# Sparse mixtures with 16-bit one-hot products and a reordered router; value products of self-attention over wide columns

## The chip, the cores and the metric

One Trainium2 chip, one core. The metric is the device time of one execution of the whole program in microseconds; the time before is the median of three runs, 3148.82 us (3148.0 to 3151.92).

## The reference

x has 2048 tokens (32 x 64) of 256 features. Four layers follow one another, each a cross-attention, a token mixer and a feed-forward part, each added to x. The change touches three of these twelve parts:

```
L0 feed-forward: shared SwiGLU (256 -> 512 -> 256) + 8 such experts, each token goes to the best 2
    probs = softmax(LN(x) @ wg.T); topw, sel = top_k(probs, 2); topw /= sum(topw)
    out = shared(x) + sum_e expert_w[:, e] * (silu(x @ g_e) * (x @ u_e)) @ d_e
L3 feed-forward: the same form, 7 experts of 256 -> 256 -> 256, the best 3, with biases on the choice
L1 mixer: self-attention, 32 heads of 8 with 8 key/value heads: q = X @ Wq.T + bq, v = X @ Wv.T + bv (64 columns)
```

## The kernel before, in words

All tensors stay transposed in SBUF: k.x and k.h are [128, 2, 2048] f32 (feature, half, token). T = 2048 tokens are NT = 16 tiles of P = 128 or NCH = 4 chunks of CH = 512. PE is TensorE, DVE VectorE, ACT ScalarE, POOL GpSimd, SP SyncE. Each stage is a block in which every engine has its own list of instructions, written out in order, with semaphores between them; a block ends when all engines have arrived.

`sparse_experts` (called by `moe_top2` for L0 with M = I/P = 4 hidden tiles, and by `moe_top3` for L3 with M = 2) has three blocks.

**The router's block** (prefix `L0r_`, `L3r_`). A layer norm in four chunks (`Norm.mean`, `var` on PE, `centre`, `scale` on DVE, `squares`, `inverse` on ACT) with one PSUM bank for the means and one for the variances; `Logits` multiplies by the router's weights, `turned` transposes. PE transposes h by tokens (L828), ACT copies it (L865), SP stores it as `rows_in` (L800), then loads the experts' weights. The shared expert runs chunk by chunk in `shared_pe`: for each hidden tile a gate and an up product (L724, 2 x 2 products of 512 columns, into one of two banks; hidden tile n waits for `hidden(n-2)` to have been read), then the down product (L731). ACT makes the silu (L738), DVE the product (`shared_hidden`, L743) and the addition to x (`shared_add`, L747). Between these, DVE carries the routing in the order of the dictionary `between`: `soften` (softmax), `pick(j)` (one-hot of the j-th choice), `gather_masks`, `weigh` (the weights of the choices), `place` (a slot for each token and choice: experts' tokens lie together in blocks of 128), `own_blocks` (each block's expert), `sort_out(j)` (L951 to L953: a one-hot of the row in the block, 128 x 16 x 128, and one of the block times the destination number). PE then multiplies these one-hots (L843, f32, 16 products for each choice), which gives for each slot the number of its row; `make_lists` (L957 to L964) turns it into `token_of` and `row_of`. L0 does three chunks of the shared expert here (LATE = 3), L3 all four (LATE = 4).

**The experts' block** (`L0b_`, `L3b_`): 39 and 54 blocks of 128 rows. POOL gathers rows by `token_of` (L1032, four buffers), PE warms up with three products of ones (L1084), transposes the rows (L1049), multiplies (L1063), transposes the hidden rows (L1071), projects (L1081); POOL scatters by `row_of` (L1037). Behind the blocks come the shared chunks from LATE on, and SP reloads the first rows of the result (L1023).

**The combination** (`L0c_`, `L3c_`): PE starts with products of ones (L1159, `2 if LATE < NCH else 8`), then adds the rows of each token by diagonal matrices of the weights (L1167), DVE adds to x (L1182).

`self_attention`, block `sap_`: PE makes the values token tile by token tile (L1861, 32 products with 64 columns), then queries and keys in a loop over the chunks (L1868), ACT adds biases (L1878), DVE spreads the values (L1895) over a tile that POOL has zeroed (L1883).

Of the kernel before, what the change touches and what calls it, by code (L numbers as in the profile page):

```python
# [20 lines left out]
ts = bass.ts  # L21
# [650 lines left out]
def sparse_experts(k, layer, E, I, top, biases):  # L672
# [7 lines left out]
    with ExitStack() as ctx:  # L680
# [10 lines left out]
        spare = sb(k, ctx, "rows", [P, max(NT * D, top * NT * P)])  # L691
# [8 lines left out]
        s_x = nc.alloc_semaphore(k.prefix + "rows_stored")  # L700
        rows_in = nc.dram_tensor(k.prefix + "rows_in", (T, D), F32, kind="Internal").ap()
# [12 lines left out]
        LATE = NCH - 1 if M > 2 else NCH  # L714

        def shared_pe(pe, sem, p_g, p_u, p_d, c, first=0):

            for m in range(M):
                n = M * (c - first) + m
                if n >= 2:  # L720
                    pe.wait_ge(sem["hidden"], n - 1)
                for w, p, made in ((wg, p_g, sem["gated"]), (wu, p_u, sem["upped"])):
                    for a in range(H2):
                        mm = pe.matmul(p[:, m % 2, :], w[:, E, a * I + m * P:a * I + (m + 1) * P], k.h[:, a, ts(c, CH)], start=a == 0, stop=a == H2 - 1)  # L724
                    mm.then_inc(made, 1)
# [25 lines left out]
        with ExitStack() as pre:  # L751
            sem = semaphores(nc, pre, k.prefix, "shifted exped step picked counted sorted listed turned copied reset gated upped silued hidden down added" + Norm.SEMS + Logits.SEMS)
# [22 lines left out]
            partf = sb(k, pre, "slot_parts_f", [P, 2, top, NT])  # L775
            oh_row = spare[:, 0:top * NT * P].rearrange("p (j t r) -> p j t r", j=top, t=NT)
            oh_block = sb(k, pre, "oh_block", [P, top, NT, NB])
# [5 lines left out]
            ln = Norm(k, pre, sem, k.x, k.h, own=(spare[:, 0:4 * CH].rearrange("p (u a c) -> p u a c", u=2, a=H2),  # L783
                                                  spare[:, 4 * CH:6 * CH].rearrange("p (u c) -> p u c", u=2), p_u[:, 0:1, :], p_u[:, 1:2, :]))
            lo = Logits(k, pre, sem, ln, w_r, (p_r[:, 0:P], p_g[:, 1, 0:P]), p_lt)
# [2786 lines left out]
```

## Time and profile before

| | |
|---|---|
| median of 3 runs | 3148.82 us |
| profiled execution | 3158.46 us, its span 3156.7 us |
| PE busy | 2778.5 us (88%), 18858 instructions |
| DVE, ACT, POOL busy | 59%, 45%, 31% |
| router, experts, combination of L0 | 500 to 605, 605 to 865, 865 to 882 us |
| values, queries, keys of L1 | 1119 to 1156 us |
| router, experts, combination of L3 | 2837 to 2928, 2928 to 3122, 3122 us to the end |

Times in rows are microseconds from the span's start. An f32 product shows as two records (passes). "PEld" is PE's weight load, "POOLq" and "SPq" are DMA issues, "PEq" is PE's sequencer.

### The profile page before, as it was taken

To read this page: it belongs to the slowest core of one execution; us is meant where nothing else is said; L and a number is where in the kernel's file an instruction comes from. 1 tells how busy PE (TensorE), PEld (TensorE's weight loads), DVE (VectorE), ACT (ScalarE), POOL (GpSimd) and SP (SyncE) were. 2 spreads that over 40 slices of the span, in tenths; PEclk is the share of its full clock that TensorE was granted. 3 is DMA by queue.
4 is the path that set the end of the run, shared out by engine and by line. 5 is a ranking of instruction groups with operands and counts; after the bars stand their busy time and mean duration, and the time that the engine had idled before them with its cause. 6 is when DMAs were issued, how large, how long until landed. Compare 5 with 4: busy or idle time off the path is not lost. (4 is left out here: it accounts for less than half of the span.)

```text
span 3156.7 us, 50277 instructions
## 1 busy us (share of the span) xinstructions
PE 2778.5 (88%) x18858; PEld 1734.1 (55%) x18862; DVE 1858.3 (59%) x2486; ACT 1415.2 (45%) x2712; POOL 987.0 (31%) x831
## 2 busy tenths in 40 slices
PE   8999997999989888889989785679988888988997
PEld 5998953466556657433346432236643555544786
DVE  3555545322268737444468597768854999985332
ACT  3333344122157636322257553546666666642222
POOL 0111100033125512000045300015511999970462
PEclk9999999999999999999999987799999999999999
DMA  4000004211110000200000000000011121203224
GB/s 156 1 0 0 0 7 140 82 45 47 54 49 2 20 4 2 84 1 0 21 1 2 15 0 0 0 22 2 2 41 36 67 80 67 78 27 107 66 82 140
DMA packets 73447, 122.63 MB, mean 39 GB/s; under 512 B 11616, under 2 KB 54240, under 8 KB 72736
## 3 DMA queue, kind: packets, MB, share of 16 engines
q1 hardware_dynamic: 64320, 95.48, 9.1%
q0 software_dynamic: 8928, 24.39, 2.4%
q8 instruction: 138, 2.26, 0.3%
q14 instruction: 61, 0.50, 0.1%
HBM read 101.10 MB, written 18.74 MB: 38 GB/s over the span
## 5 line engine op out<-in xcount | busy, mean ns | idle before, releaser
L3308 POOL TENSOR_TENSOR h<-ssm_u,ss_bc 128x1024 f32<-128x1024 f32 x88 | 205.7, 2357 | 0.0
L3271 ACT ACTIVATE ssm_p_h<-ss_delta,ss_decay 128x256 f32<-128x256 f32 x352 | 146.6, 464 | 123.8 <-DVE ctxT L3345 82.8
L3218 PE MATMUL ssm_p_y<-ctxT,ident 128*128 128x512 f32 x412 | 187.7, 595 | 0.0
L650 POOL TENSOR_TENSOR xw_prob<-xw_prob,xw_rsum 128x512 f32<-128x512 f32 x64 | 65.9, 1041 | 356.6 <-DVE xw_rsum L631 356.6
L3340 DVE TENSOR_TENSOR_SCAN ssm_p_h<-ssm_p_h,h 128x1024 f32<-128x1024 f32 x64 | 145.8, 2279 | 8.9 <-ACT ssm_p_h L3271 6.9
L3298 POOL TENSOR_TENSOR ctxT<-ctxT,ss_bc 128x1024 f32<-128x1024 f32 x50 | 117.4, 2356 | 19.2 <-DVE ctxT L3338 19.2
L500 PEld LDWEIGHTS xw_p_q<-h,xw_m_h 128*128 128x128 f32 x1024 | 116.8, 192 | 8.9 <-issue 8.9
L509 PEld LDWEIGHTS xw_p_q<-xw_u,xw_vo_h 128*128 128x128 f32 x1024 | 115.5, 192 | 10.3 <-ACT xw_u L580 10.3
L3218 PEld LDWEIGHTS ssm_p_y<-ctxT,ident 128*128 128x128 f32 x412 | 76.5, 192 | 79.4 <-issue 78.3
L509 PE MATMUL xw_p_q<-xw_u,xw_vo_h 128*128 128x128 f32 x1024 | 118.3, 276 | 0.0
L3202 PE MATMUL ssm_p_h<-ssm_b_diagonal,ssm_uT 128*128 128x128 f32 x640 | 83.1, 285 | 39.9 <-DVE ctxT L3345 19.5
L500 PE MATMUL xw_p_q<-h,xw_m_h 128*128 (+1 forms) x1024 | 117.0, 275 | 1.3 <-PEq L60 1.3
L2342 ACT ACTIVATE lmm_hidden<-lmm_p_h,vecs 128x512 f32<-128x512 f32 x64 | 43.6, 687 | 156.0 <-PE lmm_p_h L2302 108.1
L3202 PEld LDWEIGHTS ssm_p_h<-ssm_b_diagonal,ssm_uT 128*128 128x128 f32 x640 | 78.0, 197 | 63.8 <-issue 55.2
L1125 DVE TENSOR_TENSOR L0f_hidden<-L0f_silu,L0b_p_u 128x512 f32<-128x512 f32 x39 | 26.8, 688 | 122.6 <-PE L0b_p_u L1063 85.7
L621 DVE TENSOR_TENSOR xw_prob<-xw_p_s,xw_mask_bias 128x512 f32<-128x512 f32 x64 | 44.0, 688 | 91.7 <-PE xw_p_s L518 91.7
L2371 DVE TENSOR_TENSOR lmm_hidden<-lmm_hidden,lm_weights 128x512 f32<-128x512 f32 x64 | 44.1, 689 | 89.8 <-ACT lmm_hidden L2342 89.8
L1759 POOL MEMSET L3x_vx<- 128x1024 f32 x1 | 1.0, 952 | 298.5 <-POOLq L60 298.5
L1785 POOL TENSOR_TENSOR L2x_prob<-L2x_prob,L2x_rsum 128x896 f32<-128x896 f32 x64 | 65.4, 1044 | 73.5 <-DVE L2x_rsum L1722 73.5
L1785 POOL TENSOR_TENSOR L3x_prob<-L3x_prob,L3x_rsum 128x896 f32<-128x896 f32 x64 | 65.4, 1043 | 72.4 <-DVE L3x_rsum L1722 72.4
L1785 POOL TENSOR_TENSOR L1x_prob<-L1x_prob,L1x_rsum 128x896 f32<-128x896 f32 x64 | 65.4, 1044 | 71.8 <-DVE L1x_rsum L1722 71.8
L1032 POOL DMA_INDIRECT L3b_x<-L3f_rows_in,L3f_token_of x54 | 52.5, 973 | 107.9 <-POOLq L60 91.0
(845 smaller groups left out, 7175.7 us busy)
## 6 DMA issues: line engine op xcount, KB each, us to landing
ss_bc<-ss_bc_rows SPq DMA_DIRECT2D x24, 896.0 KB, 4.3
ss_bc<-ss_bc_rows SPq DMA_DIRECT2D x8, 768.0 KB, 4.1
L3f_rows<-L3f_rows_out SPq DMA_DIRECT2D x16, 384.0 KB, 4.0
L0f_wg<-in_L_ffn_gate SPq DMA_DIRECT2D x9, 512.0 KB, 10.1
L0f_wu<-in_L_ffn_up SPq DMA_DIRECT2D x9, 512.0 KB, 10.0
L0f_wd<-in_L_ffn_down SPq DMA_DIRECT2D x9, 512.0 KB, 10.0
L0f_rows<-L0f_rows_out SPq DMA_DIRECT2D x16, 256.0 KB, 3.5
x<-in_xT SPq DMA_DIRECT2D x1, 2048.0 KB, 7.5
```

The lines of the kernel that those rows point to most:

```text
L500: mm = pe.matmul(p_q5[:, q % 2, h % 4 // 2, :, h % 2, :], m_h[:, h, a, :], k.h[:, a, ts(i, P)], start=h % 4 == 0 and a == 0, stop=a == H2 ...
L509: mm = pe.matmul(p_q[:, 0, ts(o, P)], vo_h[:, h, ts(o, P)], us[:, h, :], start=h == 0 and o == 0, stop=h == NH - 1, skip_group_check=True)
L650: g.tensor_tensor(prob[:, part, :], prob[:, part, :], bcast(rsum[:, 1, part], 2, S2), ALU.mult).then_inc(sem["normed"], 1)
L1032: g.indirect_dma_start(out=xb[:, b % RX, :], out_offset=None, in_=rows_in[:, :], in_offset=bass.IndirectOffsetOnAxis(ap=token_of[:, b:b + ...
L1785: scaled = g.tensor_tensor(prob[:, m % 4, :, :, s0:s1], prob[:, m % 4, :, :, s0:s1], bcast(rsum[:, 1, m % 4, seg, :, :], 3, s1 - s0), ALU. ...
L2371: v.tensor_tensor(hh[:, m % 2, j, :], hh[:, m % 2, j, :], wb[:, j, ts(c, CH)], ALU.mult).then_inc(sem["weighed"], 1)
L3202: mm = pe.matmul(p_h[:, n % 2, e * CT + b * P:e * CT + b * P + P], uT[:, c % 2, b, ts(e, P)], db[:, i, b, :], start=True, stop=True, skip_ ...
L3218: mm = pe.matmul(p_y[:, 2 * half:2 * half + 2, :].rearrange("p e t -> p (e t)"), k.ident[:, :], weighed[n % RING_W][:, ts(half, CH)], star ...
L3271: i = act.activation(out[:, ts(e, CT)], delta[:, e, ts(c, CT)], ACT.Exp, scale=decay[:, E4 * s + e:E4 * s + e + 1])
L3298: g.tensor_tensor(tiles(weighed[n % RING_W]), tiles(weighed[n % RING_W]), bcast(bcs[:, row_c(s), :], 1, E4), ALU.mult).then_inc(sem["weigh ...
L3308: g.tensor_tensor(tiles(drive[n % RING]), u[:, c % 2, :, :], bcast(bcs[:, row_b(s), :], 1, E4), ALU.mult).then_inc(sem["driven_g"], 1)
L3340: v.tensor_tensor_scan(slot, factor, term, 0.0, ALU.mult, ALU.add).then_inc(sem["scanned"], 1)
```

## The change

In the router's block:
- The norm has two PSUM banks for means and two for variances, and the order of its steps differs.
- DVE's order is: `soften`, all picks, `gather_masks`, hidden 0, `count`, hidden 1, `place` (both parts of the old `place`), and then, for L0: hidden 2, `own_blocks`, hidden 3, add 0, `sort_rows(0)`, hidden 4, `sort_blocks(0)`, hidden 5, `sort_rows(1)`, hidden 6, `sort_blocks(1)`, hidden 7, `weigh`, add 1, hidden 8 to 11, `make_lists`, add 2. For L3: add 0, hidden 2, `sort_rows(0)`, hidden 3, `sort_blocks(0)`, add 1, `sort_rows(1)`, hidden 4, `sort_blocks(1)`, `sort_rows(2)`, hidden 5, `sort_blocks(2)`, `make_lists`, `own_blocks`, add 2, `weigh`.
- PE asks for the masks (`ranks`) after the first gate and up product.
- One-hots are bf16. The destination number is no longer one f32 factor: two bf16 marks stand in its place, the row in the tile (DVE) and the tile's number (POOL), so a listing product is bf16 with 2 x NB columns. `make_lists` puts the two together.
- The listing products stand ahead of the third chunk's down product (for L3 the third choice's behind it).
- `make_lists` makes `token_of` first and signals it; POOL issues the first four gathers here. Their buffers and semaphores belong to the whole mixture now.

L3's fourth shared chunk runs behind its blocks (LATE = 3 for both). Warming products: three ahead of the blocks for L3 alone, two ahead of the combination for both. In self-attention the values are eight products of 512 columns with the 64 weight columns as the stationary side, two token chunks side by side in the output's partitions, copied by ACT and transposed by PE (eight transposes); the loop over chunks is written out.

```diff
-        LATE = NCH - 1 if M > 2 else NCH
+        LATE = NCH - 1
...
-            p_id = p_r[:, 3 * P:3 * P + NB]
+            p_id = p_r[:, 3 * P:3 * P + 2 * NB].rearrange("p (n b) -> p n b", n=2)
...
+            partb = sb(k, pre, "slot_parts_b", [P, 2, top, NT], BF16)
+            countb = sb(k, pre, "counts_b", [P, P], BF16)
+            tiles = sb(k, pre, "tile_numbers", [P, top, NT])
+            oh_row = spare[:, 0:HOTS].bitcast(BF16).rearrange("p (j t r) -> p j t r", j=top, t=NT)
...
-            ln = Norm(k, pre, sem, k.x, k.h, own=(..., p_u[:, 0:1, :], p_u[:, 1:2, :]))
-            lo = Logits(k, pre, sem, ln, w_r, (p_r[:, 0:P], p_g[:, 1, 0:P]), p_lt)
+            ln = Norm(k, pre, sem, k.x, k.h, banks=2, own=(..., p_u, p_g))
+            lo = Logits(k, pre, sem, ln, w_r, (p_r[:, 0:P], p_d[:, 1, 0:P]), p_lt)
...
             def _(pe):
                 ln.mean(pe, 0)
                 ln.mean(pe, 1)
+                ln.mean(pe, 2)
                 ln.var(pe, 0)
-                ln.mean(pe, 2)
+                ln.mean(pe, 3)
                 ln.var(pe, 1)
-                ln.mean(pe, 3)
+                ln.var(pe, 2)
                 pe.wait_ge(s_r, n_r)
                 lo.products(pe, 0)
-                ln.var(pe, 2)
+                ln.var(pe, 3)
...
+                def listing(j):
+                    pe.wait_ge(sem["sorted"], j + 1)
+                    pe.wait_ge(sem["numbered"], j + 1)
+                    for t in range(NT):
+                        mm = pe.matmul(p_r[:, 3 * P:3 * P + 2 * NB], oh_row[:, j, t, :], marks[:, j, t, :, :].rearrange("p n b -> p (n b)"), ...)
...
                 for c in range(LATE):
                     if c == 0:
                         pe.wait_ge(sem["copied"], NT // 2)
+                    for m in range(M):
+                        shared_gate_up(pe, sem, p_g, p_u, c, m)
+                        if c == 0 and m == 0:
+                            ranks()
+                    if c == 2:
+                        for j in range(2):
+                            listing(j)
+                    shared_down(pe, sem, p_d, c)
+                    if c == 2 and top == 3:
+                        listing(2)
...
             def _(g):
+                for j in range(top):
+                    g.wait_ge(sem["based"], j + 1)
+                    g.tensor_tensor(marks[:, j, :, 1, :], base[:, j % 2, :, :], bcast(tiles[:, j, :], 2, NB), ALU.mult).then_inc(sem["numbered"], 1)
+                g.wait_ge(s_x, 16 * NT // 2)
+                g.wait_ge(sem["lists"], 1)
+                for b in range(RX):
+                    g.indirect_dma_start(out=xb[:, b, :], ..., ap=token_of[:, b:b + 1] ...).then_inc(s_b[b], 16)
...
             def _(v):
+                def sort_rows(j):
+                    v.tensor_tensor(oh_row[:, j, :, :], bcast(partb[:, 0, j, :], 2, P), bcast(countb[:, :], 1, NT), ALU.is_equal)
+                def sort_blocks(j):
+                    v.tensor_tensor(base[:, j % 2, :, :], bcast(partb[:, 1, j, :], 2, NB), bcast(countb[:, 0:NB], 1, NT), ALU.is_equal).then_inc(sem["based"], 1)
+                    v.wait_ge(sem["based"], j + 1)
+                    v.tensor_scalar(marks[:, j, :, 0, :], base[:, j % 2, :, :], dest[:, 0, 0:1], None, ALU.mult).then_inc(sem["sorted"], 1)
...
                 ln.centre(v, 0)
                 ln.centre(v, 1)
+                ln.centre(v, 2)
                 ln.scale(v, 0)
-                ln.centre(v, 2)
+                ln.centre(v, 3)
+                chain(v.tensor_scalar(tiles[:, :, :], dest[:, :, :], dest[:, 0, 0:1], 1.0 / P, ALU.subtract, ALU.mult))
+                v.tensor_copy(countb[:, :], counts[:, :])
...
...
-                keep_warm(pe, k, p_g[:, 0, :], 3)
+                if top == 3 and LATE < NCH:
+                    keep_warm(pe, k, p_g[:, 0, :], 3)
...
-            keep_warm(pe, k, p_c[:, 0, :], 2 if LATE < NCH else 8)
+            keep_warm(pe, k, p_c[:, 0, :], 2)
...
+                def values(half):
+                    for a in range(H2):
+                        for j in range(2):
+                            mm = pe.matmul(p_vc[ts(j, S), half, :], wv[:, a, :], k.h[:, a, ts(2 * half + j, CH)], start=a == 0, stop=a == H2 - 1, skip_group_check=True)
+                def turn_values(half):
+                    for t in range(4):
+                        mm = pe.transpose(p_v[:, half, :, t, :], v_cols[:, half, ts(t, P)], k.ident[:, :])
-                for half in range(2):
-                    for t in range(NT // 2):
-                        for a in range(H2):
-                            mm = pe.matmul(p_v[:, half, t, :], k.h[:, a, ts(NT // 2 * half + t, P)], wv[:, a, :], ...)
+                values(0)
+                values(1)
+                for c in range(NCH):
+                    project(c, 0, wq)
+                    project(c, 1, wk)
+                    if c < 2:
+                        turn_values(c)
```

The other edits only move definitions, or are the calls in DVE's order given above.

## Rows read from the trace of the kernel before

**Rows 1.** Timeline of PE, end of L0's experts' block (start, length, engine, line):

```profile
855.60 7.03 PE L731 MATMUL L0b_p_xh<-L0f_hidden,L0f_wd 128*128 128x512 f32 x16
...
864.87 1.95 PE L78 MATMUL L0c_p_c<-ones 128*128 128x512 f32 x4 [2.23 <-PEq L60]
```

**Rows 2.** Timeline, norm of L0's router; in brackets idle before and releaser:

```profile
503.21 1.06 ACT L207 ACTIVATE L0f_rows<-h 128x1024 f32<-128x1024 f32 x1 [2.00 <-DVE h L194]
...
503.23 1.98 PE L181 MATMUL L0r_p_u<-x,mean_ones 128*128 128x512 f32 x4 [1.31 <-DVE h L194]
...
507.47 0.67 ACT L213 ACTIVATE L0f_rows<-L0r_p_u,eps 128x512 f32<-128x512 f32 x1
...
508.83 1.23 DVE L200 TENSOR_TENSOR h<-h,L0f_rows 128x1024 f32<-128x1024 f32 x1 [2.36 <-ACT L0f_rows L215]
...
522.54 0.64 PE L234 MATMUL L0r_p_g<-h,L0f_w_r 128*32 128x128 f32 x16 [1.86 <-DVE h L200]
```

**Rows 3.** Timeline, shared chunks of L0:

```profile
559.60 1.98 PE L724 MATMUL L0r_p_g<-h,L0f_wg 128*128 128x512 f32 x4 [1.45 <-DVE L0f_hidden L743]
...
574.78 2.28 DVE L951 TENSOR_TENSOR L0f_rows<-L0r_slot_parts_f,L0f_counts 128x2048 f32<-128x2048 f32 x1
```

**Rows 4.** Tile L0r_p_r, weight loads of the listing (ns min/median/max, first and last start):

```profile
L843 PEld LDWEIGHTS L0r_p_r<-L0r_oh_block,L0f_rows x64: 190/192/333, 593.6 to 601.7; 128*128 128x128 f32 x64
```

**Rows 5.** Timeline, from L0's lists to its first expert product:

```profile
603.64 0.17 DVE L964 TENSOR_SCALAR L0f_token_of<-L0r_listed_i 128x39 int32<-128x39 int32 x1
...
605.21 5.40 PE L78 MATMUL L0b_p_g<-ones 128*128 128x512 f32 x6 [3.07 <-PEq L60]
...
609.90 0.95 POOL L1032 DMA_INDIRECT L0b_x<-L0f_rows_in,L0f_token_of  x1 [0.30 <-issue]
...
611.42 1.98 PE L1063 MATMUL L0b_p_g<-L0f_wg,L0b_xT 128*128 x4 [0.59 <-issue]
```

**Rows 6.** Timeline, L3 from its first shared product to its first expert product:

```profile
2867.78 1.96 PE L724 MATMUL L3r_p_g<-h,L3f_wg 128*128 128x512 f32 x4 [0.77 <-ACT L3f_rows L865]
...
2911.09 3.62 PE L731 MATMUL L3r_p_d<-L3f_hidden,L3f_wd 128*128 128x512 f32 x4 [3.14 <-DVE L3f_hidden L743]
...
2914.54 10.82 PE L843 MATMUL L3r_p_r<-L3r_oh_block,L3f_rows 128*128 128x54 f32 x96
...
2933.43 1.13 PE L1063 MATMUL L3b_p_g<-L3f_wg,L3b_xT 128*128 x4 [0.60 <-DVE L3b_xT L1118]
```

**Rows 7.** Timeline, end of L3:

```profile
3109.67 1.13 PE L1081 MATMUL L3b_p_y<-L3f_wd,L3f_hidden 128*128 x4 [0.71 <-DVE L3b_y L1133]
...
3114.02 2.49 SPq L1023 DMA_DIRECT2D L3f_rows<-L3f_rows_out  x5
...
3122.19 9.01 PE L78 MATMUL L3c_p_c<-ones 128*128 128x512 f32 x16 [11.39 <-PEq L60]
...
3131.04 21.60 PE L1167 MATMUL L3c_p_c<-L3c_diag,L3f_rows 128*128 128x128 f32 x192
```

**Rows 8.** Timeline, a two-input product on GpSimd, L1's attention:

```profile
1156.17 4.04 POOL L2017 TENSOR_TENSOR sam_qx<-sa_q,head_of 128x512 f32<-128x512 f32 x4 [32.74 <-SPq L1899]
```

**Rows 9.** Groups by line (busy us, mean ns; idle before), 16-bit weight load, layer 2:

```profile
L2710 PEld LDWEIGHTS f_p_g<-f_h_rounded,f_weights 128*128 128x128 bf16 x128 | 14.7, 116 | 26.8 <-issue 18.4
```

**Rows 10.** DMA issues, 604 to 614 us (count, median us to landing):

```profile
L0b_x<-L0f_rows_in,L0f_token_of POOLq DMA_INDIRECT x5, 2.7
```

**Rows 11.** Windows of VectorE in L3's router: `weigh`; `own_blocks` with one hop:

```profile
2885.85:2888.68 2.83, 2.49 (x11) 1.00 0.31 98
2904.60:2906.08 1.48, 1.38 (x5) 1.00 0.00 0
```

**Rows 12.** Timeline: four transposes; means on 32 columns; L1's value products:

```profile
619.92 0.60 PE L1071 MATMUL L0b_p_xh<-ident,L0f_hidden 128*128 128x128 f32 x4
...
882.29 1.92 PE L1214 MATMUL L1x_p_v<-x,mean_ones 128*32 128x512 f32 x16 [1.18 <-PEq L60]
...
1119.23 7.33 PE L1861 MATMUL sap_p_v<-sa_wv,h 128*128 128x64 f32 x64 [0.99 <-PEq L60]
```

More of the change, by code:

```diff
@@ L712, in sparse_experts, with shared_gate_up, shared_down @@
         n_r = 80 + 16 * len(biases or ())
[L714 to L725 removed]
+        LATE = NCH - 1
+        def shared_gate_up(pe, sem, p_g, p_u, c, m, first=0):
+            n = M * (c - first) + m
+            if n >= 2:
+                pe.wait_ge(sem["hidden"], n - 1)
+            for w, p, made in ((wg, p_g, sem["gated"]), (wu, p_u, sem["upped"])):
+                for a in range(H2):
+                    mm = pe.matmul(p[:, m % 2, :], w[:, E, a * I + m * P:a * I + (m + 1) * P], k.h[:, a, ts(c, CH)], start=a == 0, stop=a == H2 - 1)
+                mm.then_inc(made, 1)
+        def shared_down(pe, sem, p_d, c, first=0):
             if c > first:
@@ L751, in sparse_experts @@
         with ExitStack() as pre:
-            sem = semaphores(nc, pre, k.prefix, "shifted exped step picked counted sorted listed turned copied reset gated upped silued hidden down added" + Norm.SEMS + Logits.SEMS)
+            sem = semaphores(nc, pre, k.prefix, "shifted exped step picked counted based numbered sorted listed lists turned copied reset gated upped silued hidden down added" + Norm.SEMS + Logits.SEMS)
             lg = sb(k, pre, "logits", [P, NT, E])
@@ L992, in _, with hidden, add @@
-                make_lists()
+                def hidden(n):
+                    shared_hidden(v, sem, p_u, n)
+                def add(c):
+                    shared_add(v, sem, p_d, c)
+                soften()
+                for j in range(top):
+                    pick(j)
+                gather_masks()
+                hidden(0)
+                count()
+                hidden(1)
+                place()
+                if M > 2:
+                    hidden(2)
+                    own_blocks()
+                    hidden(3)
+                    add(0)
+                    sort_rows(0)
+                    hidden(4)
+                    sort_blocks(0)
+                    hidden(5)
+                    sort_rows(1)
+                    hidden(6)
+                    sort_blocks(1)
+                    hidden(7)
+                    weigh()
+                    add(1)
+                    for n in range(8, 12):
+                        hidden(n)
+                    make_lists()
+                    add(2)
+                else:
+                    add(0)
+                    hidden(2)
+                    sort_rows(0)
+                    hidden(3)
+                    sort_blocks(0)
+                    add(1)
+                    sort_rows(1)
+                    hidden(4)
+                    sort_blocks(1)
+                    sort_rows(2)
+                    hidden(5)
+                    sort_blocks(2)
+                    make_lists()
+                    own_blocks()
+                    add(2)
+                    weigh()
@@ L1095, in _ @@
                 for c in range(LATE, NCH):
-                    shared_pe(pe, late, p_g, p_u, p_d, c, first=LATE)
+                    for m in range(M):
+                        shared_gate_up(pe, late, p_g, p_u, c, m, first=LATE)
+                    shared_down(pe, late, p_d, c, first=LATE)
             @block.scalar
@@ new lines, in turn_values, with project @@
+                def turn_values(half):
+                    pe.wait_ge(sem["v_read"], half + 1)
+                    for t in range(4):
+                        mm = pe.transpose(p_v[:, half, :, t, :], v_cols[:, half, ts(t, P)], k.ident[:, :])
+                    mm.then_inc(sem["v_turned"], 1)
+                def project(c, n, w):
+                    if c >= 1:
+                        pe.wait_ge(sem["copied"], 2 * (c - 1) + n + 1)
+                    for o in range(H2):
+                        for a in range(H2):
+                            mm = pe.matmul(p_p[:, n, o, :], w[:, a, ts(o, P)], k.h[:, a, ts(c, CH)], start=a == 0, stop=a == H2 - 1)
+                    mm.then_inc(sem["proj"], 1)
```

113 lines of the change are left out of this document (46 added, 67 removed).

## The prediction

> **What bounds the kernel now.** I read the page first, then the table of windows, then the timeline of each stage that the diff touches, and last the DMA issues. The page's engine line, in the table above (PE busy 88% of the span), says that a microsecond of PE time, or of PE waiting, is a microsecond of the kernel. The timeline says where PE waits or works for nothing here. A product of 512 columns in f32 is two passes; 16 passes take 7.03 us, so a pass is 0.43 us and a product 0.86 [rows 1].
>
> The norm at the head of each mixture is a chain through three engines: the second mean waits 1.31 us because there is one PSUM bank and VectorE must have read it; a square is 1.06, a Ln 0.67 and an Exp much the same, a centring or scaling 1.23, and the last logits product starts at 522.54 [rows 2]. Among the shared chunks of L0, PE stops once, 1.45 us, for a hidden tile queued behind VectorE's placing; one one-hot comparison is 2.28 us [rows 3]. Then 32 listing products start at 594.0 and take 8.1 us (64 passes, 0.127 each, each with a weight load of 192 ns) [rows 4]; VectorE ends the lists at 603.81, PE starts the next block at 605.21 with six warming passes at half pace (5.40 us), and the first expert product starts at 611.42 [rows 5]. In L3, PE runs from 2867.78, stops 3.14 us behind VectorE's one-hots, lists for 10.82 and reaches the experts at 2933.43 [rows 6]. Behind L3's blocks PE has nothing: the last projection starts at 3109.67 (some 0.9 long, so it ends at 3110.6), five reloads are issued from 3114.02, the next block opens at 3122.19, sixteen warming passes cost 9.01, and the combination starts at 3131.04 [rows 7]. The block loops themselves are not changed.
>
> **The change, part by part.**
>
> *Two banks in the norm, both mixtures.* The means 0 and 1 (four passes each) run back to back from 500.0, where the first began, to 503.4, mean 2 follows at once since the centring of 0 ends at 503.2, then var 0 to 506.8. With the durations of [rows 2] and hops of 0.05 to 0.27 us: inverse 0 to 508.4, scale 0 to 509.7, centre 3 to 511.0; square 3 waits for inverse 1 and ends at 513.0; var 3 to 514.7; inverse 3 to 516.3; scale 3 to 517.6; the last logits product at 517.6 against 522.54. That is 4.9 us earlier in each mixture, all on the path because the transposes and shared products follow: **-9.8**. The two added VectorE operations (tile numbers, 16-bit counts, about 0.5 together) sit between centre 3 and scale 1, where VectorE waits for the inverse; without that cover they cost 0.5 each time.
>
> *L0, shared part.* The picks go ahead of the first hidden tile, so gate and up of tile 1 must find a free bank: VectorE has its masks about 0.3 us after PE began, PE asks for them 3.4 us after it. I walked VectorE's new queue against PE's 3.43 us per hidden tile; every hidden tile is made before PE wants its bank again. The stall of 1.45 goes: **-1.5**. Late next would be the hidden tile behind a one-hot, which has 1.5 us and more of slack in L0. The GpSimd half of the marks (624 elements; 512 take 1.01 us [rows 8], so 1.3) is done long before the listing.
>
> *L0, hand-over.* Listing: 32 single passes instead of 64. No row shows a 16-bit product this narrow. A pass of the f32 listing, bound by its weight load, is the upper bound, 0.127; below it cannot beat the 128-column transposes at about 0.11 by more than the load allows, and I leave 0.05 as the low end. The nearest row is the 16-bit weight load, 116 ns against 192 [rows 9, 4]: 0.127 x 116/192 = 0.077. So 2.5 us (1.6 to 4.1). It now stands ahead of the last down product, and the lists (five VectorE operations, 1.1 us), the four gathers (issues 1.25 apart [rows 5]) and their landing (2.7 [rows 10]) end 0.2 + 1.1 + 3.75 + 2.7 = 7.8 us after the listing; the down product takes 6.9 and its addition 1.4, so 8.3. The gathers are hidden, by half a microsecond; without that cover they cost up to 7. After the down product comes what [rows 1] show of the same step behind L0's blocks: from the end of the down product, 862.5, to 864.87, 2.4 us. From there 1.0 to the first gate product (from the end of the warming, 610.45, to 611.42 [rows 5]), plus a clock that may be at half for a while. At 864.87 two products took 1.95, full pace, after 2.4 us idle; at 605.21 they were at half pace after 3. Both ends: 0 and 2.3 us; I take 1.5. From 594.04 to 611.42 is 17.4; after it is 2.5 + 2.4 + 1.0 + 1.5 = 7.4: **-10.0**.
>
> The Trainium skill (TensorE: Matmul & The Clock Gate, "Why this matters for your kernels") advises warming PE up before work that counts, since it begins at half clock after an idle stretch. The sum with a half-clock start in both places where warming products are dropped would be about 2 us longer; the rows disagree among themselves, one start at each level.
>
> *L3, up to the experts.* Before, 2867.78 to 2933.43, 65.7 us, with four chunks. After: three chunks (36 products, 30.9), ranks 0.6, 48 listing passes at 0.077 = 3.7, together 35.3 if VectorE keeps up. VectorE has three one-hots at 2.28 and block marks of 2 us each in this part; my walk has the last hidden tile ready 0.1 to 0.7 us before PE can use it. Then lists and gathers (7.8) stand beside VectorE's queue: lists 1.8 (1.6 in L0, one operation fewer), own blocks 1.48, addition 1.25, weights 2.83 [rows 11], that is 7.4 and about 1.2 to open the next block; I take 8.8. The three warming products stay here and run at half pace, 4.3, and 1.0 to the gate product. 35.3 + 8.8 + 5.3 = 49.4: **-16.3**. One chunk (10.3) is not in this and comes back below.
>
> *L3, behind the blocks.* Before, 3110.6 to 3131.04, 20.4. After: the chunk 10.3, its addition and the opening 2.4 [rows 1], two warming products 1.8 at full pace or 3.4 at half; I take 2.3, so 15.0: **-5.4**. The reloads issued at 3114.02 must have landed, or SyncE holds the block: the block opened 8.2 us after their issue, at 3122.19, and the chunk ends at 3123.3. They are hidden; without the chunk they set the end, as now.
>
> *Self-attention values.* Before, 64 passes, 7.33 us [rows 12]. After, eight products of 512 columns on half the array's columns. The nearest row is the product on a quarter of the columns: 16 passes of 512 in 1.92, four at a time [rows 12]. Two at a time gives 16 x 0.43 / 2 = 3.4; one at a time 6.9. The eight transposes (four take 0.60 with their latency, some 0.44 in a stream [rows 12]) add 0.9, and ACT's copies and VectorE's additions lie beside the projections. 7.2 - 4.3: **-2.8** (up to +0.6).
>
> Sum: -9.8 - 1.5 - 10.0 - 16.3 - 5.4 - 2.8 = -45.8. The profiled execution took 3158.5 (span 3156.7), so it would take 3112.7; the median shown is 3148.8, 9.6 below it, and the forecast for it is **3103** us.
>
> **The rivals.**
>
> *A. VectorE or GpSimd is late again.* For it: the margins in L3 are under a microsecond, and a late hidden tile stopped PE 3.14 us there before, after which the clock fell. Against: that stop came from one-hots stacked ahead of one hidden tile, and they are spread now. Price, if the stops of before recur: 1.5 + 3.1 + about 1.7 for the clock: 3109. Beside this stands the Trainium skill (VectorE: DVE Perf Modes, "What auto-detection actually checks"): a 16-bit comparison doubles its rate only if every operand runs with step one, and here one operand repeats along the inner axis, so the one-hot would stay at 2.28. No row shows it; I keep 2.28, and had I halved it this rival would be worth half its chance.
>
> *B. Narrow and wide products save nothing per pass.* 80 listing passes at 0.127 instead of 0.077 is +4.0, wide products one at a time +3.4: 3110.
>
> *C. The gathers are exposed.* GpSimd issues them while VectorE works and the block may not close before they land. For it: SyncE's reloads seem to hold the block in [rows 7]. Price: landing or issue twice as long, +5 in each mixture: 3113.
>
> *D. Slower than before: the clock stays at 1.2 GHz.* L0's blocks (611.42 to the chunk before 862.5, over 220 us) start without warming and L3's combination (21.60 us [rows 7]) with two products instead of eight. At half clock the combination alone costs 21.6, each further microsecond of block work one more. It decides once 46 us of work run at half clock; with the combination (21.6) and the first ten of L0's 39 blocks (some 58) lost in full the time is 3103 + 80 = 3183. Against: at 605.21 the clock came back within 5.4 us of work, at 3122.19 sixteen passes took 9.01 instead of the 13.7 of half pace throughout [rows 5, 7].
>
> **How the numbers follow.** Forecast 0.60, A 0.15, B 0.10, C 0.10, D 0.03, and 0.02 for gains that are given back so that nothing is left. The range takes the low ends of the unknown costs (listing -2.2, clock -1.5 and -0.5, norm -1; some -5, and -4 for errors of my walk, 3094) and reaches past A, B and C to 3118. About 0.2% (6.3 us) is what a measurement of this kernel can tell from no change: faster 0.95, same 0.02, slower 0.03.
>
> **What would show it.** The last logits product 4.9 us earlier after each norm's start; no PE stop over 1 us among shared chunks; listing passes under 0.1 us; 7 to 8 us from L0's listing start to the gate product less the 6.9 of down; L3's chunk right behind the last projection and the combination some 15 us after it; wide value products in under 4 us. It is wrong if either next block opens later than 2.4 us after VectorE's last addition, if PE stops for marks or one-hots, or if half clock lasts over 5 us at a start.

## The result and the profile after

Four runs gave a median of 3104.99 us (3102.46 to 3109.57), the kernel before 3150.37 (3148.0 to 3160.66) beside them: a ratio of 0.9851, 95% interval 0.9826 to 0.9877, some 45 us. The forecast was 3103 (3094 to 3118). The profiled execution took 3109.57, span 3107.8, PE busy 2746.9 us (88%). Two single executions further down (3159.98 us of L3's chunk back, 3163.50 of no warming in L3, granted clock 0.92 and 0.91) belong to a slower state and are left out of medians and ratios.

Timeline, L0, from the listing to the first expert products (start, us, engine line operation, idle before and who ended it), against [rows 4, 5]:

```profile
583.34 1.34 PE L848 MATMUL L0r_p_r<-L0f_rows 128*128 128x78 bf16 x32
...
584.52 7.10 PE L736 MATMUL L0r_p_d<-L0f_hidden,L0f_wd 128*128 128x512 f32 x16
...
585.62 0.18 DVE L998 TENSOR_SCALAR L0f_token_of<-L0r_listed_i 128x39 int32<-128x39 int32 x1
...
586.68 1.14 POOL L903 DMA_INDIRECT L0f_x<-L0f_rows_in,L0f_token_of  x1 [24.40 <-DVE L0f_token_of L998]
...
590.64 0.95 POOL L903 DMA_INDIRECT L0f_x<-L0f_rows_in,L0f_token_of  x1 [0.30 <-issue]
591.66 1.22 DVE L752 TENSOR_TENSOR x<-x,L0r_p_d 128x1024 f32<-128x1024 f32 x1 [5.08 <-PE L0r_p_d L736]
594.96 1.28 ACT L1171 ACT_TABLE_LOAD   x1 [12.54 <-PEq L60]
595.15 0.66 PE L1117 MATMUL L0b_p_xh<-ident,L0f_x 128*128 128x128 f32 x2 [3.52 <-PEq L60]
...
596.40 3.78 PE L1131 MATMUL L0b_p_g<-L0f_wg,L0b_xT 128*128 x4 [0.60 <-DVE L0b_xT L1189]
```

The 32 listing passes take 1.34 us, 0.04 each, where 64 took 8.1. The first gather is issued 0.88 us after the list `token_of` is made. The block opens (ScalarE's table load is its first instruction) 4.3 us behind the last gather's issue and 2.1 behind VectorE's addition. Four gate passes then take 3.78 us, half pace. Of this stage's 12.9 us the listing gave 6.9 (from its start to the next operation 8.11 before, 1.18 now), the stall among the shared chunks some 1.5, and the way from there to the gate product, without the down product that now lies in it, 4.5 (9.27 before, 4.78 now).

Timeline, L3, the same place, against [rows 6]:

```profile
2881.77 1.92 DVE L990 TENSOR_SCALAR L3f_rows<-L3f_rows,L3f_dest 128x864 bf16<-128x864 bf16 x1
2881.81 1.63 POOL L899 TENSOR_TENSOR L3f_rows<-L3f_rows,L3r_tile_numbers 128x864 bf16<-128x864 bf16 x1 [4.09 <-DVE L3f_rows L988]
2883.75 0.95 PE L848 MATMUL L3r_p_r<-L3f_rows 128*128 128x108 bf16 x16 [0.94 <-DVE L3f_rows L990]
...
2890.91 0.94 POOL L903 DMA_INDIRECT L3f_x<-L3f_rows_in,L3f_token_of  x1 [0.30 <-issue]
2895.02 1.28 ACT L1171 ACT_TABLE_LOAD   x1 [18.42 <-PEq L60]
2895.05 4.25 PE L78 MATMUL L3b_p_g<-ones 128*128 128x512 f32 x6 [10.36 <-PEq L60]
```

PE waits 0.94 us for VectorE's mark before the last listing, then 10.36 us for the next block. The listing's passes take some 2.4 us in all instead of 10.8, and the stop of 3.14 us has become the 0.94.

Timeline, end of L3, against [rows 7]; chunk and reloads now lie beside each other:

```profile
3066.56 1.13 PE L1149 MATMUL L3b_p_y<-L3f_wd,L3f_hidden 128*128 x4 [0.70 <-DVE L3b_y L1204]
...
3070.91 2.49 SPq L1093 DMA_DIRECT2D L3f_rows<-L3f_rows_out  x5
...
3078.02 1.22 DVE L752 TENSOR_TENSOR x<-x,L3b_p_xh 128x1024 f32<-128x1024 f32 x1 [2.67 <-PE L3b_p_xh L736]
...
3080.37 1.95 PE L78 MATMUL L3c_p_c<-ones 128*128 128x512 f32 x4 [2.39 <-PEq L60]
3082.16 2.06 PE L1238 MATMUL L3c_p_c<-L3c_diag,L3f_rows 128*128 128x128 f32 x17
```

Read off PE's timeline at the same marks in both profiled executions, stage by stage (us):

| stage | before | changed | difference | forecast |
|---|---|---|---|---|
| norm L0, first mean to first shared product | 30.04 | 26.77 | -3.3 | -4.9 |
| L0, from there to the first gate product of the blocks | 81.42 | 68.52 | -12.9 | -11.5, with the clock |
| L0's blocks, to the last projection | 228.62 | 230.79 | +2.2 | (in the line above) |
| L0, from there to L1 | 42.25 | 44.06 | +1.8 | 0 |
| self-attention, first value product to first score | 41.40 | 37.52 | -3.9 | -2.8 |
| norm L3 | 30.30 | 25.33 | -5.0 | -4.9 |
| L3, to the first gate product | 65.65 | 50.60 | -15.1 | -16.3 |
| L3's blocks, to the last projection | 176.24 | 166.43 | -9.8 | 0 |
| last projection to combination | 21.37 | 15.60 | -5.8 | -5.4 |
| all the rest | | | +2.8 | 0 |

The sum is -48.9, as the spans say. The lines that are not the change's own work differ from execution to execution. Between the second traces of both kernels (below; spans 3152.2 and 3107.2 us, -45.0) the norms give -5.0 each, L0 -13.1, L3 -15.1 and the end -5.5, much as here; but L3's blocks give +6.7 instead of -9.8, self-attention -2.3 instead of -3.9, and all the rest -7.7 instead of +2.8.

### The profile page after: what moved, and what is told of

The parts are those of the page before. It is cut to its first block and busy times, and to the rows that moved or that the text cites. A ratio compares the mean times of both kernels' runs of the same rounds, so it can differ in the third digit from the quotient of the medians.

```text
span 3107.8 us, 49980 instructions
## 1 busy us (share of the span) xinstructions
PE 2746.9 (88%) x18724; PEld 1708.9 (55%) x18724; DVE 1863.8 (60%) x2492; ACT 1414.8 (46%) x2714; POOL 993.6 (32%) x836
## 5 line engine op out<-in xcount | busy, mean ns | idle before, releaser
L509 PEld LDWEIGHTS xw_p_q<-xw_u,xw_vo_h 128*128 128x128 f32 x1024 | 115.8, 192 | 10.7 <-ACT xw_u L580 10.2
L1105 POOL DMA_INDIRECT L0f_rows_out<-L0b_y,L0f_row_of x39 | 38.5, 986 | 146.7 <-DVE L0b_y L1204 146.7
```

The lines of the kernel that those rows point to most:

```text
L509: mm = pe.matmul(p_q[:, 0, ts(o, P)], vo_h[:, h, ts(o, P)], us[:, h, :], start=h == 0 and o == 0, stop=h == NH - 1, skip_group_check=True)
```

## The experiments

Each kernel ran five or six times beside the kernel before, and the kernel before as an experiment of its own twelve times. Its executions lie as much as 22 us apart (3151.84 to 3173.45 beside the first four), so the stages of the traces decide below, and the ratios only say where the whole stands. The runs take back the norm, the values and the place of L3's chunk; none brings back the f32 listing or VectorE's old order. What those are worth in L0 and L3 rests on the two pairs of traces, which agree to about 0.2 us.

| kernel | median us | ratio to before, 95% |
|---|---|---|
| changed, again | 3111.34 | 0.9837 (0.9814 to 0.986) |
| gathers late | 3113.69 | 0.9838 (0.9817 to 0.9858) |
| two gathers | 3112.70 | 0.9838 (0.9817 to 0.9859) |
| three warming products in L0 | 3111.67 | 0.9831 (0.9811 to 0.9851) |
| norm with one bank | 3117.15 | 0.9869 (0.9848 to 0.989) |
| old values | 3108.09 | 0.984 (0.9819 to 0.986) |
| L3's chunk back | 3112.86 | 0.9853 (0.9828 to 0.9878) |
| marks on VectorE | 3103.07 | 0.9826 (0.9805 to 0.9846) |
| before, again | 3152.78 | 0.9992 (0.9979 to 1.0006) |
| less held | 3098.10 | 0.9816 (0.9798 to 0.9834) |
| less held, no warming in L3 | 3098.14 | 0.9813 (0.9796 to 0.983) |
| less held, one gather | 3099.48 | 0.9821 (0.98 to 0.9843) |

### Both kernels again

No edit. 

> The changed kernel unaltered, as the mark for the others. Expected 3105 us, 45 to 46 less than the kernel before. Two things are open: the first six passes of L0's norm and the first gate products of L0's blocks ran at half clock in the profiled execution. If that is fixed by the kernel, both recur (six passes near 7 us where full pace gives 5.4; the gate product near 3.8 us); if it is a matter of the single execution, at least one is gone. And the kernel before's profiled execution was some 9 us above its median, in waits for transposed rows inside L3's block loop: those waits should not be in this trace (PE 20.0 of 20 us in every window there).

> The kernel before, unaltered, profiled again. In the traces so far L3's block loop, from the first gate product to the last projection, takes either 166.4 us or 171 to 176: in the longer ones VectorE and ScalarE both stand still for 1.9 us and more with their inputs ready, twice or three times. Theory (a disturbance of the single execution, in either kernel): this profile's loop lies between 166 and 177 whatever the code, and the difference of the profiled executions, 48.9 us, has up to 9.8 of it. Rival (the change itself took the pauses away): 176 again here, 166 in every trace of a changed kernel; the traces of the first four experiments with 171 to 173.5 already speak against it.

Measured: L3's blocks took 173.3 us in the changed kernel's second profile (166.43 in its first) and 166.56 in the second of the kernel before (176.24 in its first). The 9.8 us of that line are no work of the change. Timeline of the changed kernel again, one of its two long pauses:

```profile
2978.09 0.97 POOL L1100 DMA_INDIRECT L3f_x<-L3f_rows_in,L3f_token_of  x1 [0.30 <-issue]
2980.06 0.37 ACT L1180 COPY L3f_hidden<-L3b_p_xh 128x256 f32<-128x256 f32 x1 [2.54 <-remote]
2980.08 0.42 DVE L1196 TENSOR_TENSOR L3f_hidden<-L3f_silu,L3b_p_u 128x256 f32<-128x256 f32 x1 [3.56 <-remote]
...
2980.98 1.12 PE L1131 MATMUL L3b_p_g<-L3f_wg,L3b_xT 128*128 x4 [1.89 <-DVE L3b_xT L1189]
```

ScalarE and VectorE stand with their inputs made (PE's last product for them began at 2977.84) and start again within 0.02 us of each other; PE loses 1.9. Such pauses, one to three of them, are in 5 of the 14 traces, of either kernel: the first of the kernel before and the first four of the list of experiments. A pause can also bring the clock down: behind the first one of the kernel before the granted clock is 0.57 in the four us from 2972, 1.00 before and after. Of the two half-clock places the norm's was the execution's (three later traces show it too, the rest do not): the first 12 passes take

```profile
499.94 5.39 PE L181 MATMUL L0r_p_u<-x,mean_ones 128*128 128x512 f32 x12 [1.65 <-PEq L60]
```

full pace, and L0's norm 25.08 us instead of 26.77, -5.0 against before. The half clock at the start of L0's blocks recurred (block loop 230.32 against 228.62).

### When does the next block open: gathers late, two gathers

```diff
-                for b in range(RX):
+                for b in range(n):
                     g.indirect_dma_start(out=xb[:, b, :], ...
...
-                    if RX <= b < NB:
-                        g.wait_ge(sem["turned_x"], b - RX + 1)
+                    if n <= b < NB:
+                        if b >= RX:
+                            g.wait_ge(sem["turned_x"], b - RX + 1)
```

The first lines stand in the router's block, the others in the experts' block; n is 0 and 2.

Late: 

> The first four gathers go back into the experts' block, all else as in the changed kernel. Theory (the router's block is held by outstanding gathers, about 4.2 us from the last one's issue to the opening): L0's experts' block opens 2.4 us after the end of the last down product instead of 3.7, L3's 0.5 us earlier; but the first gate product then waits 6.2 us from the opening, as before, instead of 1.3 in L0 and 5.1 in L3. Sum -1.3 + 4.9 - 0.5 + 1.1 = about +4.2 us on the changed kernel. Rival (an opening 3.7 us after the down product is what a block costs, gathers or not): openings stay, +6.0 us. Second rival (gathers landed in the shadow in either place): +1 or less.

Two: 

> Two of the four gathers stay in the router's block, the other two are issued first in the experts' block. Theory (held by gathers): the last issue in the router's block comes 2.5 us earlier, so the opening is set by VectorE's last operation again, 2.3 to 2.4 us after it: -1.3 us in L0, about -0.5 in L3, the first gate products as much earlier, and nothing lost since blocks 2 and 3 are wanted over 5 us later. Sum -1.8 us, near what the comparison can tell; the place of the opening in the trace decides. Rival (not held by gathers): openings stay, 0 us.

Timeline with the gathers late, start of L0's blocks:

```profile
593.96 1.28 ACT L1168 ACT_TABLE_LOAD   x1 [12.00 <-PEq L60]
594.71 1.14 POOL L1097 DMA_INDIRECT L0f_x<-L0f_rows_in,L0f_token_of  x1 [32.88 <-POOLq L60]
...
597.71 0.66 PE L1114 MATMUL L0b_p_xh<-ident,L0f_x 128*128 128x128 f32 x2 [6.55 <-DMA L0f_x<-L0f_rows_in,L0f_token_of]
```

The block opens 1.5 us after VectorE's addition (591.20 + 1.22), but PE waits for the row: from the down product's start to the gate product 14.9 us against 11.7, +3.3; in L3, where warming products cover the landing, -0.2. Together +3.0, the theory had 4.2. With two gathers, same stage:

```profile
585.26 0.95 POOL L903 DMA_INDIRECT L0f_x<-L0f_rows_in,L0f_token_of  x1 [0.30 <-issue]
...
588.79 1.22 DVE L752 TENSOR_TENSOR x<-x,L0r_p_d 128x1024 f32<-128x1024 f32 x1 [5.08 <-PE L0r_p_d L736]
591.41 1.28 ACT L1172 ACT_TABLE_LOAD   x1 [11.86 <-PEq L60]
```

L0 opens 0.7 us earlier, 1.4 behind VectorE; L3 opens 1.5 earlier (1.4 behind VectorE's last operation) and its gate product comes 0.7 earlier, since the warming products took 5.03 instead of 4.29. So the gathers do hold the block. Over all traces of changed kernels the opening is the later of two: 1.2 to 1.5 us behind VectorE's last operation, and 4.0 to 4.4 behind the last gather's issue. The second is no price of its own kind. The semaphore that tells of the last gather's landing rises 2.7 to 2.9 us after its issue in each of these traces, and where the gather holds the block the opening follows 1.2 to 1.6 us after that, about as long as it follows VectorE's last operation. The block closes when its last work, a landing included, is done. Tile L0f_x of the changed kernel, 584 to 593 us, its four gathers:

```profile
DMA to landing us min/median/max: 2.7/2.8/3.0
```

### Warming products at the start of the blocks

In L0 (three put back, `keep_warm(pe, k, p_g[:, 0, :], 3)` for both mixtures): 

> Three warming products stand again at the start of L0's experts' block. Theory: they take 4.3 us at half pace as in L3, and buy back the 2.1 us that the first gate and up products lost to half clock: +2.1 us on the changed kernel. Rival (warming pays, as the Trainium skill advises): what they save in the first block is 4 us or more, 0 or less in sum. Second rival (the first gathers would have been waited for anyway): 0.

```profile
594.82 4.41 PE L78 MATMUL L0b_p_g<-ones 128*128 128x512 f32 x6 [3.45 <-PEq L60]
...
600.14 1.98 PE L1131 MATMUL L0b_p_g<-L0f_wg,L0b_xT 128*128 x4 [0.59 <-DVE L0b_xT L1188]
```

The gate products are at full pace and the block loop takes 228.62 again; from the opening to the last projection 234.0 us against 231.5 in the changed kernel again (232.2 in its first trace): +1.8 to +2.5, as expected. In L3, where the same three were left out, it came out differently (below).

### Norm with one bank

Banks, own tiles and the order of all engines as in the diff's removed lines. 

> The norm at the head of both mixtures with one PSUM bank for the mean and one for the variance and the old order of work on all engines; all else as changed. Theory from the two traces: +3.3 us in L0 (its first means were at half clock in the changed kernel, which gave part of the gain back) and +5.0 in L3, sum +8.3. The prediction's own sum: +9.8. Rival (the two banks only moved a wait behind the logits): +3 or less.

Measured: L0's norm 30.04 us, L3's 30.93, against 25.07 and 25.33 at full clock: +5.0 and +5.6. The prediction's -4.9 each was right; the -3.3 on which the expectation rested was the clock of one execution. Banks and order went back together, so the run does not say which of them carries the 5 us.

### Old values

`sap_` as before the change. 

> Self-attention's values computed as before, in 64 passes of 64 columns straight into token order; all else as changed. Theory from the two traces: +3.8 us (41.4 against 37.6 from the first value product to the first score). The prediction's term: +2.8. Rival (wide products one at a time on half the array): 0.

```profile
1106.54 7.33 PE L1932 MATMUL sap_p_v<-sa_wv,h 128*128 128x64 f32 x64 [0.99 <-PEq L60]
```

The first score starts at 1148.38, 41.8 us behind it; in the changed kernel again 39.15: 2.7. The wide products (16 passes) take 3.65 us, the transposes add 0.43 us for each four. The 3.8 of the expectation held 1.6 us of warming products behind the projections, which ran at full pace in 5 of the 14 traces and near half in the others (2.81 against 4.2 to 4.5 us). From the first value product to those warming products the clock plays no part: 36.96 us in both traces of the kernel before, 37.40 here, 34.48 or 34.78 with the wide products. That is 2.2 to 2.5 between the kernels and 2.6 to 2.9 against this run, so the prediction's 2.8 stands, at its upper end.

### L3's chunk back

```diff
-        LATE = NCH - 1
+        LATE = NCH - 1 if M > 2 else NCH
...
-                    own_blocks()
                     add(2)
+                    hidden(6)
+                    own_blocks()
+                    hidden(7)
                     weigh()
+                    add(3)
```

with 8 warming products ahead of the combination. 

> L3's fourth shared chunk goes back into the router's block, behind the listing, with eight warming products ahead of the combination; all else as changed, so own blocks and weights now lie beside that chunk. Theory: behind the blocks 20.4 us as before instead of 14.7, +5.7; up to the experts one chunk longer (10.3) but without the 7.4 us of VectorE's work after the listing in the open, about +3. Sum +8.7 us. Rival (the chunk behind the blocks brings nothing by itself, the gain was all in the hand-over): +3. Rival (moving the chunk is worth all of 10 us because the experts' loop starts earlier): +10 or more.

Measured: first shared product to first gate product 53.4 us against 50.6, +2.8; last projection to combination 21.3 against 15.6, +5.7. Sum 8.5, as the theory had it.

### Marks on VectorE

```diff
-                    g.tensor_tensor(marks[:, j, :, 1, :], base[:, j % 2, :, :], ...
+                    v.tensor_tensor(marks[:, j, :, 1, :], base[:, j % 2, :, :], ...
```

The product moves from GpSimd's list into VectorE's `sort_blocks`.

> Both block marks on VectorE, GpSimd makes none; all else as changed. In the trace of the changed kernel VectorE's mark (a 16-bit product with a scalar, 624 elements) took 1.46 us in L0 and 1.92 us (864 elements) in L3, each begun in the same moment as GpSimd's product. Theory (the two engines hold each other up): VectorE's mark alone takes 0.3 to 0.7 us, and the second product some 0.8 to 1.2, so VectorE's queue is about as long as before and the kernel within 1 us of the changed one. Rival (the mark costs 1.5 to 1.9 us by itself): VectorE has 1.2 to 1.6 us more for each of five marks, late in L3: +4 us.

Groups by line of VectorE in L0's shared part, 540 to 590 us (busy us, mean ns), first of the changed kernel:

```profile
L990 DVE TENSOR_SCALAR L0f_rows<-L0f_rows,L0f_dest 128x624 bf16<-128x624 bf16 x2 | 2.9, 1456 | 0.1
```

then of this one:

```profile
L988 DVE TENSOR_TENSOR L0f_rows<-L0f_rows,L0r_tile_numbers 128x624 bf16<-128x624 bf16 x2 | 1.6, 800 | 0.0
L987 DVE TENSOR_SCALAR L0f_rows<-L0f_rows,L0f_dest 128x624 bf16<-128x624 bf16 x2 | 0.8, 388 | 0.1
```

The same mark takes 388 ns alone and 1456 beside GpSimd's product (447 and 1922 with 864 elements in L3). Both marks on VectorE are shorter than one beside GpSimd, and PE's stop of 0.94 us in L3's router is gone (first shared product to the last listing 33.29 us, 34.22 before).

### Less held by the gathers and the weights

```diff
-                    make_lists()
                     own_blocks()
+                    make_lists()
                     add(2)
-                    weigh()
...
+                weigh()
                 for c in range(LATE, NCH):
```

Beside both marks on VectorE and two gathers in the router's block; the last lines are VectorE's in the experts' block, where the weights are now made ahead of the late chunk's hidden tiles, in L0 too.

> Both marks on VectorE, two gathers in the router's blocks, the weights moved behind the experts' blocks, L3's own blocks ahead of the lists. Theory: L3's router block is held first by VectorE's last operation (it opens 1.4 us behind it) and by the last gather's issue (4.1 us behind it). VectorE ends some 4 us earlier; the second gather is issued some 3 us earlier than the fourth was. So L3's first gate product comes 3.5 us earlier than with the marks alone changed, L0's 0.7; the weights cost nothing behind the blocks (2.8 us beside 3.4 of gate and up). Against the changed kernel: the listing stop of 0.9 gone, sum -5.1 us. Rival (the weights stand before the chunk's hidden tiles and stop PE there): behind L3's blocks 15.6 us becomes 17 or more. Rival (PE's clock needs its time from the restart, so an earlier start is given back in the warming products): half of the 3.5 is lost.

```profile
2881.01 0.96 POOL L900 DMA_INDIRECT L3f_x<-L3f_rows_in,L3f_token_of  x1 [0.30 <-issue]
2885.04 1.28 ACT L1158 ACT_TABLE_LOAD   x1 [14.79 <-PEq L60]
```

L3's opening is held by the gather alone, 4.0 us behind its issue. From the last listing to the gate product 13.8 us, against 16.8 with the marks alone changed: -3.0 (3.5 expected). On the changed kernel it is -3.5 from the first mean to the gate product in L3 (72.4 us, 75.9 before) and -0.7 at L0's opening, 4.2 of the 5.1 expected. Last projection to combination stays at 15.6: the weights cost nothing there. The median of 3098.1 is the lowest of all; its ratio lies below the changed kernel's in either of its series, though the intervals overlap.

One gather: 

> As the version with both marks on VectorE, late weights and early own blocks, but with only one gather in each router's block. Theory (a block opens at the later of 1.4 us after VectorE's last operation and 4.0 us after the last gather's issue): in L3 the hold by gathers moves 1.3 us forward, so PE starts 1.3 us earlier than at two gathers, the warming products cover the second gather's issue and landing; L0 is held by VectorE already and stays. Sum -1.3 us on the version with two. Rival (the second block's row lands late): a PE stop of 1 us or more before the second block's transposes, in L0 (no warming there) above all, sum 0 or above.

Measured: the opening is 1.4 us earlier (7.22 instead of 8.60 behind the last listing's start), still 4.0 behind the gather's issue (2880.43, 2884.44), and no row was late. The gate product is 0.7 earlier only: the warming products took 5.04 instead of 4.36. The median shows nothing of it.

No warming in L3: 

> As the kernel beside it, and L3's three warming products left out too. Theory: they take 4.3 to 5 us; without them the first gate product follows the opening by 1.0 to 1.3 us, and the first gate, up and down products run at half clock for about 2 us: -2 us on the kernel beside it, -7 on the changed kernel. Risk in its favour being lost: the third and fourth gathers are issued 0.6 and 1.9 us after the opening and land 3 us later, while blocks 2 and 3 are wanted at about 7 and 10 us, so no wait. Rival (warming pays in L3): the block loop is 4 us or more longer and the sum is 0 or above.

```profile
2886.03 2.07 PE L1118 MATMUL L3b_p_g<-L3f_wg,L3b_xT 128*128 x4 [0.60 <-DVE L3b_xT L1191]
...
2890.83 2.07 PE L1118 MATMUL L3b_p_g<-L3f_wg,L3b_xT 128*128 x4 [0.60 <-DVE L3b_xT L1191]
...
2895.70 1.12 PE L1118 MATMUL L3b_p_g<-L3f_wg,L3b_xT 128*128 x4 [0.60 <-DVE L3b_xT L1191]
```

The theory failed. The gate product comes 3.8 us nearer to the opening, but the first two blocks run at half pace, for 9.7 us, and the block loop takes 169.8 us instead of 166.1. The sum is 0: in L3 warming and not warming cost the same.

## Why the prediction was right, point by point

- **Norm, -9.8**: right to 0.1 in each mixture wherever the clock was full (25.07 and 25.33 us against 30.04 and 30.30). In the profiled execution of L0 the means began at half clock, which no term held, and gave 1.7 back.
- **L0, shared part and hand-over, -11.5**: came to -12.9 + 2.2 = -10.7 (-13.1 + 1.7 = -11.4 in the second pair of traces). Two terms were mis-sized against each other.
  The listing was put at 2.5 us (0.077 a pass) and took 1.2 (584.52 less 583.34), below my low end of 1.6. One part of the miss is a misread row: the 0.127 a pass that I scaled from [rows 4] mixes two clocks. In the kernel before, the f32 passes start 0.112 apart at full clock, in L0 and in L3, and the last eight of L0's 64 start 0.213 apart, because the granted clock fell while they ran. Windows of the kernel before, the clock is the third number from the end:

```profile
598.00:600.00 2.00, 2.00 (x21) 2.00 (x20) 0.00 (x0) 0.00 (x0) 0.00 (x0) 1.00 0.00 0
600.00:602.00 2.00, 2.00 (x12) 2.00 (x11) 0.00 (x0) 0.00 (x0) 0.00 (x0) 0.54 0.00 0
```

  So PE was at half clock before its 3 us of idle time at 605.21 began. The other part is the scaling by the weight loads: an f32 pass takes 0.112 with 39 and with 54 columns, a 16-bit pass 0.037 with 78 and 0.049 with 108. The 16-bit passes follow their columns, the f32 ones do not, which fits a weight load that sets the f32 pass and no longer the 16-bit one.
  The opening was put at 2.4 us behind the down product, with the gathers hidden "by half a microsecond"; it was 3.5. That the block closes when they land, 2.7 us after issue [rows 10], was right. The walk put nothing between the finished list and the first gather, which took 0.9 us, and 3.75 for four issues, which took 3.96: the last landing came 8.7 us after the listing and not 7.8, VectorE's addition ended at 8.2. The opening then followed the landing by 1.6 us. The clock's 1.5 was 2.1.
- **The stall of 1.45 us** in L0's shared chunks went, and no PE stop over 1 us came among them.
- **L3, up to the experts, -16.3**: -15.1. Up to the end of the last listing it was 35.2 us (35.3 forecast): the passes gained (48 in some 2.4 us instead of 3.7), and PE stopped 0.94 for a mark, which the walk missed since it had block one-hot and mark at 2 us together, which took 3.0. VectorE then worked 7.4 us as said [rows 11], but the block opened 2.9 behind it and not 1.2, held by the last gather: its issue came 6.2 us after the listing, it landed at 9.0 where the sum had 7.8, and the block opened at 10.3 instead of 8.8.
- **L3, behind the blocks, -5.4**: -5.8, confirmed by taking it back (+5.7).
- **Values, -2.8**: 2.2 to 2.9, by the trace it is held against. They ran two at a time, as [rows 12] suggested.
- **9.6 us between the profiled execution and the median**: I subtracted them as if they were a constant. The pauses in L3's blocks do not explain them alone: the kernel before's second trace has none and its L3 blocks are 9.7 us shorter, but its execution (3153.97 us) is only 4.5 shorter, since it was 5.3 us slower elsewhere. What made up the distance stays open. Term by term the stages give some 44 us against the 45.8 of the sum; that the forecast also lies within 2 us of the measured median is in part luck, with executions of one kernel up to 22 us apart.
- **The signs of an error that I had named.** By the letter all three came: PE stopped for a mark (0.94 us in L3), half clock lasted over 5 us at a start (L0), and L3's block opened 5.6 us after VectorE's last addition, though the sum itself had put 2.83 us of the weights' work behind that addition. Beyond the terms of the sum they cost some 4 us with L0's opening; the listing, 1.3 us cheaper than forecast in each mixture, hid more than half of it. So the total was nearer than its parts.
- **Rivals.** A was half seen: VectorE's mark is late because GpSimd's product runs beside it, 0.9 us instead of 6. B fell: narrow passes cost 0.04, wide ones two at a time. C was the nearest: the gathers are exposed, 0.7 us in each mixture as the two-gather run shows, not 5. D fell, but half clock lasted 6 us in L0 and 9.7 in L3 without warming. The Trainium skill (TensorE: Matmul & The Clock Gate, "Why this matters for your kernels") says to warm up with matmuls before one is measured, since the slower clock is measured otherwise. The traces agree that first products run at half pace; whether warming products pay inside a kernel is another matter, and here they did not: leaving them out gave -2 us in L0 and 0 in L3. The Trainium skill's rule on 16-bit operands (VectorE: DVE Perf Modes, "What auto-detection actually checks") agrees with the trace: the one-hot, whose one operand repeats along the inner axis, took 2.28 us in 16 bits, as in f32.

## What to carry to other kernels

Before a gather is moved into the block before its use, find what closes that block. Here an outstanding gather held it until it had landed, 4 us from issue to the next block's opening, so only as many gathers as the first blocks need belong there. Count the step from the finished list to the first issue too (0.8 to 0.9 us). Before work is split between VectorE and GpSimd, look at what runs at the same moment: two marks one after the other on VectorE (1.2 us) were shorter than one on each engine side by side (1.5 us). Before a price per pass is taken from a total, look at the granted clock through it. And compare executions stage by stage before a microsecond is given to the change, since clock phases of 2 us and pauses that added up to 10 came and went with the execution.

## What the runs showed of the hardware

- VectorE's 16-bit product with a scalar took 388 ns alone and 1456 ns when GpSimd's 16-bit product of the same 624 elements began at the same moment (447 and 1922 at 864 elements).
- In a stream where each product has its own 128x128 weights, a 16-bit product of 78 or 108 columns costs 0.037 or 0.049 us (1.18 and 1.55 us from the first of 32 to the next operation). The f32 pass costs 0.112 at full clock, with 39 columns as with 54, and 0.213 at half.
- In both traces of the kernel before, the clock fell to half within such a stream of narrow f32 passes, some 6 us after it began and without a stop of PE; L3's stream of 96, 10.6 us long, kept its 0.112 a pass to the end.
- An indirect gather landed 2.7 to 3.0 us after its issue. Where the last gather was the last work of its block, the next block opened 1.2 to 1.6 us after the landing, 4.0 to 4.4 us after the issue; where VectorE was last, 1.2 to 1.5 us after its operation. GpSimd issued the first gather 0.8 to 0.9 us after VectorE had made its list.
- ScalarE and VectorE paused together, some 2 us with their inputs ready, in 5 of 14 traces, seen in L3's block loop and not in L0's. What both waited for stays open; no run here tells it.
- Half pace after an idle stretch lasted from some 3 us (L3's warming products from 2895.05) to 9.7 us, and the same place was at full pace in one execution and at half in another (the warming products behind the projections, 2.81 us in 5 traces, 4.2 to 4.5 in 9).
